# Attention weights stored in rows of features, and the first normalisation moved ahead of the selector on GpSimd

## The reference

```python
def reference(x, Wq, Wk, Wv, Wp, bp, ...):          # Wq, Wk, Wv: (16, 128, 64); Wp: (1024, 128)
    h = layernorm(x)
    q = einsum('bnd,hde->bhne', h, Wq) / sqrt(64)
    k = einsum('bmd,hde->bhme', h, Wk)
    v = einsum('bmd,hde->bhme', h, Wv)
    out = einsum('bhnm,bhme->bnhe', softmax(einsum('bhne,bhme->bhnm', q, k)), v)
    x = x + swapaxes(out, -1, -2).reshape(B, N, 64 * 16) @ Wp + bp
    y = layernorm(layernorm(x)) * g1 + lb1          # the second one with g1, lb1
    y = gelu(y @ ternary(w1).T + b1)
    return x + (layernorm(y) * g2 + lb2) @ ternary(w2).T + b2
```

## Time and profile before

| | |
|---|---|
| device time, median of 3 runs | 1002.18 us (1001.26 to 1003.38) |
| span of the profiled execution | 998.7 us |
| the profiled execution's own time | not recorded beside the span; the median less the span is 3.5 us |
| busy: PE, PEld | 98%, 78% |
| busy: DVE, POOL, ACT | 88%, 84%, 73% |
| the chain that ended last | PE 95%, DVE 2%, ACT 1%, POOL 1%, issue 1% |
| DMA | 57.82 MB, mean 58 GB/s; 203682 packets |

### The profile page before, as it was taken

One profiled execution on the slowest core, in us unless ns is written; L12 is line 12 of the kernel. 1 busy time (PEld: TensorE's weight loads), 2 busy tenths in 40 slices (PEclk: granted clock), 3 DMA queues, 4 the chain that ended last, 5 costly groups with the idle time before them and its releaser, 6 DMA issues.

```text
span 998.7 us, 39391 instructions
## 1 busy us (share of the span) xinstructions
PE 980.8 (98%) x16052; PEld 782.2 (78%) x16052; DVE 880.0 (88%) x1779; ACT 729.6 (73%) x1151; POOL 837.1 (84%) x861
## 2 busy tenths in 40 slices
PE   7899999999999999999999999999999999999998
PEld 6577777778777787887887777888878777788886
DVE  7888988988889888898889988889889988788998
ACT  5687677777767777777777777777777776879995
POOL 6789888989887888888899888888888889866765
PEclk9999999999999999999999999999999999999999
DMA  6112332222331232233222233324222233354343
GB/s 141 38 32 51 53 66 45 43 49 52 74 53 27 51 73 53 52 53 71 55 48 41 48 73 51 53 53 71 46 41 47 52 52 53 69 86 75 77 86 65
DMA packets 203682, 57.82 MB, mean 58 GB/s; under 512 B 185072, under 2 KB 203248, under 8 KB 203504
## 3 DMA queue, kind: packets, MB, share of 16 engines
q1 hardware_dynamic: 201424, 54.79, 29.8%
q10 hardware_dynamic: 2080, 0.52, 0.2%
HBM read 7.21 MB, written 4.19 MB: 11 GB/s over the span
## 4 chain that ended last, share of the span: by engine, by line
PE 95%; DVE 2%; ACT 1%; issue 1%; POOL 1%; DVEq 0%; POOLq 0%; ACTq 0%
PE S L675 11%; PE PV L700 8%; PE M L635 7%; PE PV L702 6%; PE PV L701 6%; PE QK L622 5%; PE QK L623 5%; PE QK L624 5%; PE misc L675 5%; PE S L667 5%; PE S L864 3%; PE M L753 2%; PE M L718 2%; PE M L754 2%; PE M L755 2%; PE misc L667 2%
## 5 line engine op out<-in xcount | busy, mean ns | idle before, releaser
L1210 POOL TENSOR_TENSOR pl<-p 128x1024 f16<-128x1024 f32 x253 | 476.9, 1896 | 39.3 <-ACT p L1000 39.1
L1410 DVE TENSOR_REDUCE negmax<-M 128x4 f32<-128x1024 f32 x252 | 306.8, 1217 | 22.4 <-PE M L635 16.4
L1008 ACT ACTIVATE QKh<-QK 128x512 f16<-128x512 f32 x251 | 149.5, 596 | 155.5 <-PE QK L624 155.3
L1000 ACT ACTIVATE p<-S,s_exp 128x1024 f32<-128x1024 f32 x173 | 192.4, 1112 | 71.8 <-PE S L675 71.2
L700 PEld LDWEIGHTS PV<-V,p 128*128 128x128 bf16 x2048 | 186.8, 98 | 46.4 <-issue 34.5
L700 PE MATMUL PV<-V,p 128*128 128x65 f16 x2048 | 214.9, 194 | 4.0 <-DVE O L1424 2.9
L701 PE MATMUL PV<-V,p 128*128 128x64 f16 x2048 | 213.4, 193 | 0.0
L702 PE MATMUL PV<-V,pl 128*128 128x65 f16 x2048 | 212.6, 194 | 0.0
L1430 DVE TENSOR_TENSOR QKl<-QK,QKh 128x512 f16<-128x512 f32 x251 | 172.4, 687 | 42.2 <-ACT QKh L1008 41.1
L701 PEld LDWEIGHTS PV<-V,p 128*128 128x128 bf16 x2048 | 189.1, 97 | 4.7
L702 PEld LDWEIGHTS PV<-V,pl 128*128 128x128 f16 x2048 | 188.7, 97 | 0.0
(11 more groups left out here) (236 smaller groups left out, 2501.6 us busy)
## 6 DMA issues: line engine op xcount, KB each, us to landing
result<-X SPq DMA_DIRECT2D x15, 256.0 KB, 2.6
X<-in_L_attn_query SPq DMA_DIRECT2D x7, 512.0 KB, 4.8
OT<-O SPq DMA_TRANSPOSE x64, 4.6
shift<-negmax SPq DMA_TRANSPOSE x63, 2.3
O<-in_L_attn_Wk ACTq DMA_DIRECT2D x2, 256.0 KB, 4.3
O<-in_L_attn_Wq SPq DMA_DIRECT2D x2, 256.0 KB, 4.5
O<-in_L_attn_Wv SPq DMA_DIRECT2D x1, 512.0 KB, 3.9
w<-in_L_ffn_w SPq DMA_DIRECT2D x2, 256.0 KB, 5.6
```

Source lines behind the costliest of these rows:

```text
L1000: e.activation(p32[r][:, :, :, :].rearrange("p i m n -> p (i m n)"), score_bank(p)[:, :], ACT.Exp, scale=s_exp[:, :]).then_inc(s_ex, 1)
L1210: e.tensor_tensor(pl[r][:, :, :, :].rearrange("p i m n -> p (i m n)"), p32[r][:, :, :, :].rearrange("p i m n -> p (i m n)"), p_high(r).rea ...
L1410: e.tensor_reduce(dst[:, :, NB * jj:NB * jj + NB], max_bank(p)[:, :].rearrange("p (i t m) -> p i t m", i=2, t=NB), AX.X, ALU.max, negate=T ...
```

## The change

The host stores `Wq`, `Wk` and `Wv` as 128 rows of 1024 (feature, then head and column) and `Wp` as 128 rows of 8x128, before the kernel is launched (`laid_out`). The same bytes then go to the same places in SBUF with runs of 2 KB (`Wq`, `Wk`, a half each) and 4 KB (`Wv`, `Wp`), and `Wp` takes one DMA on 128 partitions where it took two on 64. On POOL the normalisation of the first batch is put ahead of the two instructions that build the selector.

```diff
-        Q_IN, K_IN, V_IN, P_IN, W12_IN, FFN_IN, ROWS_IN, BP_IN = 16, 16, 16, 32, 32, 64, 32, 16
+        Q_IN, K_IN, V_IN, P_IN, W12_IN, FFN_IN, ROWS_IN, BP_IN = 16, 16, 16, 16, 32, 64, 32, 16
...
-            heads = slice(half_ * H // 2, (half_ + 1) * H // 2)
-            return e.dma_start(by_head(Wqk[:, i, :])[:, heads, :], w_in[heads].rearrange("h d e -> d h e"))
+            cols = slice(half_ * WQ, half_ * WQ + WQ)
+            return e.dma_start(Wqk[:, i, cols], w_in[:, cols])
...
-            e.dma_start(by_head(Wv), wv_in.rearrange("h d e -> d h e")).then_inc(v_in, 16)
+            e.dma_start(Wv, wv_in).then_inc(v_in, 16)
...
-            wp_v = wp_in.rearrange("(e c hh) o -> hh e c o", c=HC, hh=2)
-            for hh in range(2):
-                e.dma_start(Wp[hh * E:(hh + 1) * E, :, :], wp_v[hh]).then_inc(p_in, 16)
+            e.dma_start(Wp[:, :, :], wp_in).then_inc(p_in, 16)
...
+            norm_root(0)
+            norm_apply(0)
             e.wait_ge(s_ident, 2)
             e.tensor_tensor(sel8[:, :], ident[:, 0:2 * GP], ident[:, E:E + 2 * GP], ALU.add).then_inc(s_ident, 1)
             e.wait_ge(s_ident, 3)
             e.tensor_scalar(sel[:, :, :], sel8[:, :].unsqueeze(2).to_broadcast([P, 2 * GP, P]), SHIFT_UP, None,
                             ALU.mult).then_inc(s_sel, 1)
-            norm_root(0)
-            norm_apply(0)
...
+def laid_out(name, a):
+    if name in ("L0_attn_Wq", "L0_attn_Wk", "L0_attn_Wv"):
+        return a.transpose(1, 0, 2).reshape(D, H * E)
+    if name == "L0_attn_Wp":
+        return a.reshape(E, HC, 2, D).transpose(2, 0, 1, 3).reshape(P, HC, D)
+    return a
```

More of the change, by code:

```diff
@@ L469, in t2_rows @@
             return T[:, :, :].rearrange("p c d -> p (c d)")
-        def by_head(w):
-            return w.rearrange("p (h e) -> p h e", h=H)
         def load_half(e, i, w_in, half_):
-            heads = slice(half_ * H // 2, (half_ + 1) * H // 2)
-            return e.dma_start(by_head(Wqk[:, i, :])[:, heads, :], w_in[heads].rearrange("h d e -> d h e"))
+            cols = slice(half_ * WQ, half_ * WQ + WQ)
+            return e.dma_start(Wqk[:, i, cols], w_in[:, cols])
         x_tok = x_in.rearrange("b (t p) d -> p (b t) d", p=P)
@@ L1728 @@
     for name in _INS:
-        a = np.ascontiguousarray(inputs[name])
+        a = np.ascontiguousarray(laid_out(name, np.asarray(inputs[name])))
         arrays[f"in_{name}"] = a
```

## The result

| | before | after |
|---|---|---|
| median of 21 runs of each (us) | 1001.4 (1000.8 to 1003.4) | 1002.9 (1001.5 to 1004.3) |
| ratio after / before | | 1.0013 [1.0007, 1.0019] |
| span of the profiled execution (us) | 998.7 | 1000.5 |
| its first `queries_keys` matmul (us) | 12.04 | 13.75 |

The account below looks back on a forecast made before the run. PE was taken to bound the middle (95% of the chain), a relay the first 13 us. The held `diag` gave +0.89 us, the earlier normalisation's 0.57 included, loads 0: 1002.18 + 0.9 = 1003.1 us, range 1001.1 to 1004.7.

Parts of the forecast that it names:

- the held `diag`: DVE's `diag` beside POOL's moved selector: held until 10.42 against 9.53 before, +0.89 us; the forecast case, chance 0.42.
- The start sets the end: Everything behind the spread of the maxima waits for it; its shift is the whole price, as the full middle recovers nothing.
- The 3.5 us: Time outside the profiled span, between the shown median 1002.18 and the span 998.7 us; taken as unchanged.
- It starts at 4.12 instead of 4.69: POOL's first normalisation, moved ahead of the selector: starts earlier, batch normalised at 7.34 instead of 7.91; alone gains 0.57 us.
- the landing of 2.5 us: First input's load, issued together with the first half of `Wk`: landed in 2.5 us, so statistics are ready at 4.04.
- rival C: First input lands 1.0 us later behind `Wk`'s long runs, moving statistics through hold alike: +0.9 + 1.0, 1004.1 us; chance 0.06.
- rival B: DVE's `part_qk` also meets the running selector, held until 10.42 instead of 8.33: 1.9 us later, 1004.1 us; chance 0.24.
- The faster halves, 0: `Wq` and `Wk` loads in longer runs: 0.8 us gained, `part_qk` ready at 7.4 rather than 8.17, nothing on the path.
- `Wv` and `Wp`, 0: Loads of `Wv` and `Wp`: their readers stand behind the start's relay, so no one waits for either; 0.

Follow-up runs that it names:

- e3: After, with `Wk`'s two halves issued by SP between those of `Wq`, all behind the input, nothing issued by ACT; 1001.23 us, ratio 0.9995 to before.
- e2: After, with the selector built ahead of the normalisation again, so only the weights' layout and loads differ from before; 1002.85 us, ratio 1.0012 to before.
- e5: After, with 36 in place of 24 idle transposes while PE waits for the first batch; 1001.34 us, ratio 1.0003 to before.
- e9: After, unchanged, run again to see how much of its trace repeats; 1002.65 us, ratio 1.0008 to before.
- e10: After, with 36 idle transposes and the selector in four pieces, three ahead of the normalisation; 1001.34 us, ratio 0.9998 to before.
- e4: After, with `Wk` alone stored by head again and loaded by ACT in runs of 256 bytes; 1001.07 us, ratio 0.9994 to before.
- e7: After, with `Wk` alone stored in groups of four heads and loaded in runs of 1 KB; 1000.31 us, one run, no ratio.
- e8: The probe: before, with six added phases, each a large POOL instruction beside a row of small DVE ones; no time or ratio given.
- e1: Before, with only POOL's order changed, the normalisation ahead of the selector; 1001.96 us, ratio 1.0004 to before.
- e6: e4 with the selector's large instruction cut in four, three pieces before the normalisation and one behind; 1000.84 us, ratio 1.0000 to before.
- e12: e3 with the selector in four pieces, two ahead of the normalisation and two behind; 1000.31 us, ratio 0.9986 to before.
- e11: e1 with the selector in four pieces, three ahead of the normalisation and one behind; 1001.31 us, ratio 0.9997 to before.

## Why the number was right and the reason wasn't

The forecast was 1003.1 and slower by 0.9; 1002.9 was measured, slower by 1.5. The step that carried the forecast, the held `diag`, is not in the profiled execution of after at all. What is in it was a rival of 6% and something that the prediction doesn't mention. So it is luck that the number came close. It is luck in the base, too: 1002.18 was the median of three runs and lies 0.8 above that of 21, which made up for a loss that was forecast too small.

- **The start sets the end: right, but for the clock.** From the first `queries_keys` to the end of the span it is 986.6 to 986.8 us in before, in after and in ten of the eleven experiments beside the probe; the eleventh is e3 with 987.8 (the clock at 0.58 at 25 us). So the first 12 us of the program are the case, and with them whatever the clock does behind. The 3.5 us that the prediction puts between span and time set a median of three runs against one span; where both are on record for one run, they lie 1.8 to 2.5 apart. Nothing in the difference hangs on it.
- **"It starts at 4.12 instead of 4.69": wrong, and where the loss begins.** The free POOL gains 0.57 only if the input is there. In the five profiles in which `Wk` comes in runs of 2 KB on the other queue (after, e2, e5, e9, e10) the statistics start at 4.28 to 4.65; in the eight others at 2.89 to 3.67. The prediction held the landing of 2.5 us fixed and gave the late input, rival C, 0.06. C's price was right for the input itself (+1.0 forecast, +1.0 to 1.4 measured), not for the hold added to it. The page of the Trainium skill beside C ("DMA: Bandwidth & Descriptors", "Queues, rings and completion order") says that an engine turns to another queue only behind a packet of several descriptors. e3 and e4 agree with it; e7's 3.50 at four times the run doesn't show a delay in proportion. That it is this rule and not another cost of the long runs is not shown. I took the page for a possibility without a row, and a rule without a row needed more than 0.06, as nothing spoke against it.
- **`diag` held until the selector's end, +0.89: a true mechanism, wrongly read.** The earlier trace rows are pairs with POOL's `tensor_tensor`, and the selector is a `tensor_scalar`. Its hold has a gap: a small one that starts between 1.05 and 1.64 us behind it runs freely, and a `tensor_scalar` 128x2 that starts at 1.80 or 1.85 is held (e8 and the others). Whether `diag` falls into it depends on what stands ahead: 1.14 (e4, e7, e9) and 1.64 (after) are free, 1.80 (e1, e3, e5) is held for 1.00 us. The 1.80 is no chance: where `part_qk` meets the selector, it is let go at 1.05, and the relay from it to `diag` takes the rest. So rival B was half right: the hold of `part_qk` doesn't cost 1.9 us by itself, but brings on that of `diag`. The page of the Trainium skill that the prediction took ("SBUF — State Buffer", "SBUF: two separate sides") has the lock held for the whole instruction; e8 agrees beside a `tensor_tensor` (2.06 us) and not beside a `tensor_scalar` (0.87 to 0.99, then free).
- **The clock of PE: missing.** At the batch, the clock fell in the profiles where PE had been idle for 2.15 and 2.36 us (e2, after), and not where it had been for 1.64 or less (e1, e9 and the rest; before had 1.27). It costs 0.96 us by e9. The prediction has no term for the clock and says nothing of PE's idle time. The length of one gap isn't all that decides, though: e3's clock fell at 24 us behind a gap of 0.82 that did nothing elsewhere.
- **The faster halves, 0: right, by another way.** (The loads as a whole were not 0: they made the input late.) The rate did rise, to 411 GB/s at 4 to 5 us against 288. But `part_qk` was ready at 8.61, not at 7.4: `Wq`'s first half came later, and DVE took all four in a row from 5.95. PE asked for `part` only at 9.76, so no one waited.
- **`Wv` and `Wp`, 0: right.** The distance from the start to the end didn't change.

The sum of causes can be checked on the 87 runs of before beside the experiments and the 32 of after and e9, since each lists its span and mean clock. Their medians, too, are 1.5 apart. Where the mean clock is 0.999 or 1.000, the spans have a median of 998.8 in before (46 of 87 runs) and 999.4 in after and e9 (7 of 32): a difference of 0.6, to which the 0.53 between `queries_keys` in before and e9 answers, the late input net of the earlier normalisation. None of these seven spans (999.2 to 999.8) stands a hold's 1.0 us above the others. With the clock at 0.998 or less it is 999.9 and 1000.9. After has such a clock in 25 of 32 runs, before in 41 of 87, and 0.996 in 6 of 32 against none. So the other 0.9 of the 1.5 between the medians goes with the clock, which falls in more of the runs, and in some twice or for longer.

That it falls at the batch, as in the two profiles, is inferred for the other runs. For it speaks that e5 and e10, with 36 idle transposes, have it in 2 of 11 runs each. Against it as the only place speaks e6, with 5 of 11 behind an idle time of 0.77. Where it falls in before's runs stays open, as its profiled execution shows 1.00 throughout: at the batch, or at 24 us as in e3, where the fall cost 1.1 us, which is also what parts before's two groups (998.8 and 999.9). Before with 36 idle transposes, the run that would separate the two, was not made.

## What to carry to other kernels

A small load that the whole program waits for should be costed with what runs beside it on other queues, not with its old landing time: making its neighbours efficient may delay it, and putting it alone at the head of their queue was the cheap remedy here (statistics at 2.94 and 2.89 in e3 and e12). Before a long POOL instruction is moved into a gap, list the small DVE instructions that ran there, and check the hold with POOL's same kind of operation; cut it if they would meet. And where a change lengthens PE's wait before a serial chain, look at the granted clock behind it, in more than one profile of the same kernel, and at the mean clock of every run: a median can move by it with the start unchanged.

## What the runs showed of the hardware that was not expected

- POOL's `tensor_scalar` of 1024 elements (2.78 us) holds DVE's small instructions in two stretches, from its start to 1.05 us and, for a `tensor_scalar` 128x2, from 1.80 at the latest (1.64 is still free) to the end; POOL's `tensor_tensor` (2.12 us) in one. A `tensor_scalar` 128x1 was never seen held by itself, only behind a held one (e8). Why the two operations differ isn't shown.
- The input's 128 KB landed 3.79 us after the issue beside runs of 2 KB on the other queue (3.5 at least in e2, e5, e9 and e10), against 2.5 beside runs of 256 bytes, 2.63 in e4, where these came back, and 2.9 in e1 and e11.
- The same kernel's 24 idle transposes ended at 6.34 in one execution and at 6.84 in another (8 matmuls against 6 between 5 and 6 us, with a granted clock of 1.00 shown in both). The first then ran at 1.2 GHz from 9 to beyond 12 us and the second at 2.4; that the half microsecond decided it is likely, but not shown.
